# Low halves of the eight gate pieces made by VectorE instead of GpSimd, in a fused feed-forward and state-space kernel

## What is computed

```
x = x + 0.5 * ffn(layernorm(x))        # "ffn1"
x = x + attn(layernorm(x))             # a selective state-space block
x = x + 0.5 * ffn(layernorm(x))        # "ffn2", same weights

ffn(x):   g = (x @ gate_w.T) * gate_s;  u = (x @ up_w.T) * up_s
          return ((silu(g) * u) @ down_w.T) * down_s      # weights are -1, 0, 1
attn(x):  h, gate = split(W_in @ x)                       # 1024 channels each
          h = silu(causal_conv4(h) + conv_b)
          ts, B, C = split(Wx @ h);  each RMS-normalised  # 128, 16, 16
          delta = softplus(Wdt @ ts + dt_bias)
          s[t] = exp(delta[t]*A) * s[t-1] + delta[t]*B[t]*h[t]   # 1024 x 16 states
          y[t] = sum_n s[t,n]*C[t,n] + D*h[t];  y = y * silu(gate)
          return Wout @ y
```

## Time and profile before

| | us |
|---|---|
| median of 3 runs | 2776.47 (2773.37 to 2778.87) |
| the profiled execution, as timed | 2791.37 |
| its span, first to last instruction | 2789.4 |
| DVE busy | 2461.4 (88%) |
| PE busy | 2381.1 (85%) |
| POOL busy | 2272.8 (81%) |
| ACT busy | 1758.2 (63%) |
| mean granted TensorE clock | 0.912 of full |

### The profile page before, as it was taken

How to read it: one execution, slowest core, us unless ns; L and a number is a source line. 1 busy time by engine, 2 the same in 40 slices (tenths; PEclk the granted TensorE clock), 3 DMA queues, 4 the chain that set the end, 5 groups by cost and what they waited for, 6 DMA issues and landing times. The chain is left out here.

```text
span 2789.4 us, 38187 instructions
## 1 busy us (share of the span) xinstructions
PE 2381.1 (85%) x12266; PEld 1961.2 (70%) x12266; DVE 2461.4 (88%) x3119; ACT 1758.2 (63%) x2995; POOL 2272.8 (81%) x1393
## 2 busy tenths in 40 slices
PE   7888887888688998889988998789987984699968
PEld 6766776676467886677767887677866863577747
DVE  5679997897899998999989999999999987999972
ACT  5585677575657665675568765666667756474531
POOL 2369689789977999699987989699996999888842
PEclk9898998899789999999989999999998996599979
DMA  8754835837575577846787578856788486366634
GB/s 289 261 196 150 299 114 174 303 118 270 175 251 198 165 243 263 295 148 224 235 294 246 157 231 281 304 166 190 237 264 280 122 307 242 106 219 203 231 95 137
DMA packets 293424, 605.61 MB, mean 217 GB/s; under 512 B 23008, under 2 KB 23776, under 8 KB 293216
## 3 DMA queue, kind: packets, MB, share of 16 engines
q1 hardware_dynamic: 293216, 603.08, 64.7%
HBM read 450.42 MB, written 152.57 MB: 216 GB/s over the span
## 5 line engine op out<-in xcount | busy, mean ns | idle before, releaser
L2053 POOL TENSOR_TENSOR sbuf<-dus,bring 128x1024 f32<-128x1024 f32 x512 | 1219.8, 2396 | 175.1 <-PE pt L1489 86.1
L1658 ACT ACTIVATE pa<-dls,cst 128x512 f32<-128x512 f32 x1024 | 699.2, 690 | 498.1 <-DVE sbuf L1840 484.7
L1489 PE MATMUL pt<-ident,sbuf 128*128 128x128 f32 x4096 | 660.7, 298 | 188.3 <-DVE sbuf L1840 68.9
L1489 PEld LDWEIGHTS pt<-ident,sbuf 128*128 128x128 f32 x4096 | 537.3, 154 | 318.2 <-DVE sbuf L1840 98.2
L1407 PE MATMUL pm<-xT,wring 128*128 128x512 f32 x2816 | 712.4, 401 | 17.7 <-DVE xT L1712 9.8
L1840 DVE TENSOR_TENSOR_SCAN sbuf<-pa,carry,sbuf 128x512 f32<-128x512 f32 x512 | 635.7, 1268 | 23.4 <-ACT pa L1658 13.6
L1840 DVE TENSOR_TENSOR_SCAN sbuf<-pa,sbuf 128x512 f32<-128x512 f32 x512 | 605.9, 1207 | 34.3 <-POOL sbuf L2053 19.8
L1851 DVE SCALAR_TENSOR_TENSOR acc<-pt,cT,acc 128x512 f32<-128x512 f32 x768 | 547.5, 737 | 81.3 <-PE pt L1489 71.9
L1420 PE MATMUL pm<-wring,act 128*128 128x512 f32 x2176 | 582.4, 410 | 26.9 <-DMA wring<-wsp 8.0
L1407 PEld LDWEIGHTS pm<-xT,wring 128*128 128x128 f32 x2816 | 519.2, 190 | 120.8 <-issue 17.2
L1420 PEld LDWEIGHTS pm<-wring,act 128*128 128x128 f32 x2176 | 401.7, 193 | 114.2 <-issue 12.0
(11 more groups left out here) (153 smaller groups left out, 2283.8 us busy)
## 6 DMA issues: line engine op xcount, KB each, us to landing
wring<-wsp SPq DMA_DIRECT2D x408, 512.0 KB, 4.3
bring<-b_d SPq DMA_DIRECT2D x256, 256.0 KB, 3.9
xn_d<-tb SPq DMA_DIRECT2D x24, 1024.0 KB, 9.7
xnb<-xn_d SPq DMA_DIRECT2D x19, 1024.0 KB, 7.8
x_d<-tb SPq DMA_DIRECT2D x16, 1024.0 KB, 5.3
sg_d<-hd SPq DMA_DIRECT2D x64, 256.0 KB, 4.5
tb<-x_d SPq DMA_DIRECT2D x16, 1024.0 KB, 7.2
spw<-u_d SPq DMA_DIRECT2D x30, 512.0 KB, 4.5
```

The source lines that it names most:

```text
L1489: ins = e.matmul(pt[u.pt[tt]][:, k * P:(k + 1) * P], sbuf[:, u.s3, k, tt * P:(tt + 1) * P], ident[:, :], is_transpose=True, start=True, st ...
L1658: e.activation(pa[k % 2][:, :], dls[:, k, :], ACT.Exp, scale=col(C_A + (4 * u.ig + k) * N + u.n)).then_inc(S.a_exp, 1)
L2053: e.tensor_tensor(sbuf[:, u.s3, h * m:(h + 1) * m, :], dus[:, h * m:(h + 1) * m, :], bring[:, u.s2:u.s2 + 1, :].broadcast_to([P, m, TC]), ...
```

## The change

A unit now carries `by_pool`, which is true for the late pieces of the output projection alone. The low half of a late gate piece raises DVE's piece semaphore and is issued by DVE; POOL's program skips it. The eight `Wout` pieces stay as they are.

```diff
@@ Book.staged
         u.n, u.slot, u.k, u.there, u.before, u.late = n, slot, k, there, before, late
+        u.by_pool = late and n >= WO
         u.hi = self.up(self.S.a_piece)
-        u.lo = self.up(self.S.g_piece if late else self.S.v_piece)
+        u.lo = self.up(self.S.g_piece if u.by_pool else self.S.v_piece)
@@ dve_pieces
-                    elif u.kind in ("whole", "part") and not u.late:
+                    elif u.kind in ("whole", "part") and not u.by_pool:
                         q.wait_ge(u.hi)
                         e.tensor_tensor(staged_out(u)[:, 1, :], staged_in(u), staged_out(u)[:, 0, :],
                                         ALU.subtract).then_inc(S.v_piece, 1)
@@ pool_consts
-                    elif u.kind == "whole" and u.late:
+                    elif u.kind == "whole" and u.by_pool:
                         q.wait_ge(u.hi)
                         e.tensor_tensor(staged_out(u)[:, 1, :], staged_in(u), staged_out(u)[:, 0, :],
                                         ALU.subtract).then_inc(S.g_piece, 1)
```

## The result

| | before | after |
|---|---|---|
| median, us | 2774.92 (4 runs, 2770.57 to 2778.87) | 2796.0 (4 runs, 2794.93 to 2800.17) |
| ratio | | 1.0058, 95% interval 1.0036 to 1.0079 |
| span of the profiled execution, us | 2789.4 | 2793.9 |

The changed kernel is slower by 0.58%, about 16 us. The two medians of the table lie 21 us apart, which is 0.76% and inside the interval of the ratio. The forecast was 2777 us and no change that can be told, with a range of 2766 to 2789: wrong, and outside the range. The two profiled spans show almost nothing of it, since the first trace of before is of a run of 2791.37 us, slower than all four in the table.

A forecast was written before the change was run, and what follows sets the result against it. DVE, busy 88%, was taken to bound the kernel, PE close behind the opening, POOL in places. -0.4 + 1.8 - 1.3 + 0.5 = +0.6 us on the median 2776.5 gave 2777 us, no change; 8-in-10 range 2766 to 2789.

The forecast's parts named there:

- (a): Opening, way into dt: bn ready earlier without POOL's half, dt matmuls start at 143.8 to 144.5; gain 0.4 us.
- (b): Six of the eight halves on DVE in the opening: hidden in DVE's idle time, cost 0.
- (c): Last two halves on DVE between the gate product behind dus and the first scan: cost 1.8 us, at most 4.6.
- (d): Softplus steps on DVE in the opening, no longer held beside POOL's two halves: gain 1.3 us, bounds 0 to 3.1.
- (e): Gates 6 and 7 on PE start later, PE waits about 10 us, xT 6 to 9 us later: cost 0.5 us.
- The slower rival: PE enters 190 to 240 us late and DVE waits for it: 7.6 us, 2784 us; chance 0.24.
- (f): Rest of the program, same work in slightly different interleaving: taken as 0, with 8 us each way.
- The faster one: Recurrence two steps ahead relieves POOL, one of DVE's long waits gone: about -7.5 us, 2769 us; chance 0.20.
- The third rival: Move does nothing for PE, reshuffle decides: either sign, within 8 us around 2777; chance 0.07 slower beyond 5.6 us, 0.07 faster.

The follow-up runs named there:

- e3: Kernel before with DVE making the eight halves, the last two right where ACT had delivered their high halves, all else in the old order; ratio 0.9994.
- e1: Kernel before with DVE making the eight halves at the changed kernel's places, all else in the old order; ratio 1.0021.
- e2: Changed kernel's new order for everything else, but POOL makes the eight halves as in the kernel before; ratio 1.0051.
- g6: Kernel before, halves on POOL, with the changed kernel's order only between scans 288 and 352 (about 900 to 1050 us); ratio 1.0062.

## Why the prediction was wrong, point by point

**(a), the way into dt: right in size.** The dt matmuls start at 143.57 against 144.50, 0.2 us ahead of the forecast of 143.8 to 144.5, and after a wait for `tsT` as forecast. PE was 0.65 us earlier in this trace from its first gates on, so the gain is 0.3 to 0.9 us.

**(b), six halves hidden: right.** The wait of 12.00 us became one of 6.84 us and short ones, and the softplus steps did not move back.

**(c), the last two halves: the term was mis-sized.** I took 1.8 us from the shorter cases of the earlier trace rows, with 4.6 as the top, and it was 5.22, above even that. All eight in the changed kernel (shortest, median, longest ns):

```profile
L1880 DVE TENSOR_TENSOR wring<-tb,wring x8: 691/1197/2850, 127.8 to 170.4; 128x512 fp32r<-128x512 f32 x8
```

The longest, 2850 ns, stood beside POOL's products of 2.6 us each (three in 7.91 us). The Trainium skill (SBUF — State Buffer, "Who interferes with whom") has an instruction of VectorE with two SBUF inputs and one of GpSimd that reads SBUF exclude each other for the whole instruction. The trace agrees: 0.68 us where POOL did nothing or was only about to begin (e3), and 2.85 us beside its products. I had held that rule and priced it in a sentence beside the sum, and it should have been the term.

**(d), the softplus steps: right.** 1.22 + 2.77 + 1.21 = 5.2 us against 2.29 + 2.79 + 1.69 = 6.77 us, a gain of 1.6 where 1.3 was taken. The middle one is as long as before and stands beside POOL's 3.20 us product at 161.50; the two that had stood beside halves are back at 1.2 us. (c), 5.22 us, was three times this gain.

**(e), gates 6 and 7 later: right in kind and nearly in size.** PE waits 11.50 us (forecast about 10), starts gate 6 at 170.55 (169.7), and the last `xT` of the chunk ends at 190.4 against 180.6, 9.8 us later (6 to 9). Scan 0 is 3 us later (forecast within 1 of 170.6): that is (c). I took 0.5 us for all of (e). By e1 against e3, (c) and (e) together cost 1.0021 - 0.9994 = 0.27% or 7.5 us, known to some 6 us either way, where the sum had 2.3 us for both. The two traces have e1 behind e3 by 2.9 us at scan 0, 4.1 at scan 64 and 2.2 at scan 352, hardly more than the 2.9 us that (c) makes ahead of scan 0. So (c) was too small in the sum, and whether (e) was stays open. The slower rival's sign did not come: DVE is busy for 25.00, 24.73 and 25.00 of 25 us in the three stretches from 190 to 265 us.

**(f), the rest of the program: the step that failed.** "I take 0 and keep 8 us each way", on two waits of DVE. It was the largest term: e2 has it at +0.51%, 14 us, above the bound. The loss appeared between scans 284 and 412, 16 to 19 us of it by the start of scans, in two about equal parts by DVE's work. From 900 to 1050 us before has DVE at 98% and PE at 99%, and there the new order lost 6 us of DVE's work; from 1050 to 1200 us, where before has waits too, it lost 6 to 9 us more. The two waits of the earlier trace rows priced neither: a stretch without waits has nothing for a new order to win and can only lose, and where an engine waits already it can wait longer. So the ends of (f) were not alike on both sides: gains are bounded by the idle time of the engine that decides, losses are not. g6, which is back in the old order behind scan 352, still loses in the second part; whether its first part or its cut (6.3 us between scans 352 and 356) does this stays open. The test set for (f), scans within 3 us of each other up to 500 us, failed too: scan 96 leads by 5.5 us, scan 128, at 507 us, by 13.7.

**The rivals.** The faster one came true as a mechanism, up to scan 128: DVE did 83.79 us of work in 400 to 500 us instead of 75.72, and e2 (81.86 us) shows that the order did this and not the lighter POOL. Of the earlier trace rows the wait at 485 us was gone, and the one at 658 us was 5.86 us long. At scan 284, 887 us, the kernels that began with the new order led by 1.5 to 7.8 us (7.5 was the price), the changed one by 6.4, and the stretch behind took 17.8 us from it. The third rival, that the reshuffle decides, is what happened; I gave its costly end 0.07 and a size of 5.6 to 8 us, and it had 14. The sum that gave 2777 us was off by 3.4 us in (c) and by some 14 us in (f), which had no row behind it.

## What to carry to other kernels

Where a program's order comes from a greedy planner, a change of one instruction's engine draws a new order for everything behind it. Here three such draws cost 0.45, 0.51 and 0.71% with nothing else changed; for another kernel that says only that the size is to be measured. So price the reshuffle as a cost of its own, look at the stretches where two engines are both full and not at the long waits alone, and try an edit with the old order kept word for word (e1, e3) before it is judged. An instruction moved to VectorE belongs where its input becomes ready and GpSimd rests: the same two subtractions took 1.4 us at one place and 5.22 us at another. Look at the neighbours too: in e3 2.2 us of the holding fell on the next DVE instruction, and 2.9 us were left of the 3.9.

## What the runs showed that was not expected

- A subtraction of 128x512 floats on DVE took 0.68 us alone and up to 2.85 us beside GpSimd products of 128x1024 (2.6 us each).
- The cost of an order is not a sum over stretches: g2 (new up to scan 288, 1.002) and g3 (new from 288 to 416, 1.0058) together exceed e2 (1.0051), by 0.27%, which the intervals alone do not set apart from nothing; the traces show a part of it, the cut from the new order back to the old, 9.9 us at scan 288 in both kernels that have it. What stands in those 9.9 us stays open.
- Runs of one and the same program spread by 0.7% (the kernel before: 2773.17 to 2792.01 us in 30 runs), so two traces can differ by 15 us with nothing changed; a step shared by several traces is what can be trusted.
